# First layer of a two-layer image network: 42 of the 170 hidden channels get a TensorE pointwise product and nine VectorE depthwise taps, and the stacked rows are copied by DMA

## The reference, cut to what matters

```python
h = jnp.einsum('oi,bihw->bohw', w_in, x)             # 64 -> 3 * 170 channels
gate, x_sp, x_fr = jnp.split(h, 3, axis=1)
sp = conv_general_dilated(x_sp, w_dw, ..., padding='SAME', feature_group_count=170)   # 3x3, one filter a channel
f  = jnp.fft.rfft2(x_fr in 8x8 patches) * fft_weight
fr = jnp.fft.irfft2(f)
fused = jax.nn.gelu(gate) * (sp + fr)
out = jnp.einsum('oi,bihw->bohw', w_out, fused)      # 170 -> 64 channels, added to x
```

## Time and profile before

| what | value |
|---|---|
| time, median of 3 runs | 11264.19 us (11263.31 to 11265.12) |
| profiled execution, its own time | 11251.14 us |
| its span, first to last instruction | 11249.3 us |
| mean granted TensorE clock | 0.973 |
| TensorE matmuls busy | 10537.8 us (94%), 62242 instructions |
| VectorE busy | 7718.4 us (69%), 11335 instructions |
| ScalarE busy | 5114.5 us (45%) |
| GpSimd busy | 2503.7 us (22%) |
| DMA queue of SyncE | 1334.39 MB, 41.6% of 16 engines |

### The profile page before, as it was taken

One profiled execution on the slowest core, in us unless ns is written; L12 is line 12 of the kernel. 1 busy time (PEld: TensorE's weight loads), 2 busy tenths in 40 slices (PEclk: granted clock), 3 DMA queues, 4 the chain that ended last, 5 costly groups with the idle time before them and its releaser, 6 DMA issues.

```text
span 11249.3 us, 161094 instructions
## 1 busy us (share of the span) xinstructions
PE 10537.8 (94%) x62242; PEld 7829.9 (70%) x62242; DVE 7718.4 (69%) x11335; ACT 5114.5 (45%) x7799; POOL 2503.7 (22%) x2340
## 2 busy tenths in 40 slices
PE   1999998999899999998989999999998999999998
PEld 1777775767677776675767777667676777757666
DVE  6555558888655555897855555688884555578787
ACT  0333334656633333464753333445474333345557
POOL 0111112233211111323321111222332111122333
PEclk6999999999999999999999999999999999999999
DMA  4333325465533333546543333444563222253555
GB/s 124 62 74 63 71 57 209 158 225 144 133 71 63 75 64 103 185 158 224 146 114 63 70 64 73 144 160 182 187 169 72 56 58 53 55 191 147 203 165 149
DMA packets 1203095, 1344.68 MB, mean 120 GB/s; under 512 B 829196, under 2 KB 1062044, under 8 KB 1100060
## 3 DMA queue, kind: packets, MB, share of 16 engines
q1 hardware_dynamic: 1202332, 1334.39, 41.6%
HBM read 787.50 MB, written 515.26 MB: 116 GB/s over the span
## 4 chain that ended last, share of the span: by engine, by line
issue 42%; PE 37%; DVE 10%; POOL 8%; ACT 2%; DMA 1%; SPq 0%; POOLq 0%; DVEq 0%; ACTq 0%
PE ps L1637 12%; POOL xo L983 7%; PE ps L1650 6%; PE ps L1228 4%; PE ps L1664 3%; PE ps L1255 3%; DVE S L1426 3%; PE ps L1221 2%; PE ps L1659 2%; PE ps L1292 2%; DVE fp L1395 2%; DVE rs L1215 1%; DVE fx L1386 1%; ACT fp L1349 1%; PE ps L796 1%
## 5 line engine op out<-in xcount | busy, mean ns | idle before, releaser
L983 POOL TENSOR_SCALAR xo<-xo 64x512 f32<-64x512 f32 x504 | 783.6, 1578 | 4848.2 <-DVE xo L1078 4848.2
L904 ACT ACTIVATE XF<-ps 128x340 f32<-128x340 f32 x1024 | 465.6, 455 | 2865.4 <-PE ps L760 2865.3
L1637 PE MATMUL ps<-fp,Dwr 128*128 128x512 f32 x6144 | 1471.4, 389 | 0.0
L1637 PEld LDWEIGHTS ps<-fp,Dwr 128*128 128x128 f32 x6144 | 1153.4, 188 | 239.4
L1042 DVE TENSOR_TENSOR Z<-ps,LW 128x340 f32<-128x340 f32 x1024 | 524.3, 512 | 1105.5 <-PE ps L769 1097.8
L806 PE MATMUL ps<-P,WP 128*106 128x512 f32 x3072 | 934.7, 439 | 0.0
L796 PE MATMUL ps<-H,WP 128*128 128x512 f32 x3072 | 924.2, 423 | 0.0
L1078 DVE TENSOR_TENSOR xo<-ps,raw 64x512 f32<-64x512 f32 x512 | 351.9, 687 | 812.0 <-PE ps L849 808.5
L1228 PEld LDWEIGHTS ps<-RS,Bc 128*128 128x128 f32 x4096 | 570.6, 195 | 483.9 <-DVE RS L1217 241.5
L1228 PE MATMUL ps<-RS,Bc 128*128 128x128 f32 x4096 | 762.7, 310 | 144.2 <-DVE RS L1217 144.2
L1650 PE MATMUL ps<-XP,Cwr 128*128 128x512 f32 x3072 | 832.2, 408 | 68.1 <-DVE XP L1769 68.1
(11 more groups left out here) (294 smaller groups left out, 21146.5 us busy)
## 6 DMA issues: line engine op xcount, KB each, us to landing
raw<-x SPq DMA_DIRECT2D x240, 640.0 KB, 8.3
fx_d<-fx SPq DMA_DIRECT2D x112, 1024.0 KB, 3.9
fl_d<-fp SPq DMA_DIRECT2D x112, 1024.0 KB, 5.4
fp<-fl_d SPq DMA_DIRECT2D x112, 1024.0 KB, 6.1
fx<-fx_d SPq DMA_DIRECT2D x112, 1024.0 KB, 5.5
x1h_d<-xo SPq DMA_DIRECT2D x256, 256.0 KB, 8.3
x1v_d<-xo SPq DMA_DIRECT2D x512, 128.0 KB, 5.0
xin<-x1v_d SPq DMA_DIRECT2D x64, 1024.0 KB, 4.8
```

Source lines behind the costliest of these rows:

```text
L904: e.activation(XF[n % 2][:], ps[6][:, 0:2 * HID], ACT.Copy).then_inc(sem["xf"], 1)
L983: ins = e.tensor_scalar(dst, src, 1.0, None, ALU.mult)
L1637: ins = e.matmul(bank(m)[:], Dwr[:, w, c:c + 128], fq[n % 2][x][:, s2, :], start=(s2 == 0 and w == 0 and x == 0), stop=False)
```

## The change

The pointwise product of the 42 channels is no longer multiplied by the taps in advance. `pointwise` makes it once for the ten rows that a tile needs (nine rows of 130 columns in each half of the partitions): three pieces of 106 x 390, each of three matmuls, into PSUM banks 0, 1 and 5, which the gates use too. ScalarE copies them into a new SBUF tile `U` (`uc`). VectorE makes nine taps in `F42` (`depthwise`: one multiplication, then eight scalar_tensor_tensor that add onto the same tile, each of which waits for the one before). `finv42` has bank 4 for itself, and `fu42` becomes two instructions, the second waiting for the first: add the bank to `F42`, then multiply by the gate.

`pairs` is gone from VectorE. SyncE copies the two halves of `Hh` from `P` by two DMAs a tile (`load_h_rows`). `pointwise` of tile t + 1 stands in tile t, where `conv42` stood, and so do the first two blocks of the 128-channel `conv`, which need no `Hh`. On VectorE `p2(t + 2)` stands behind `fu42(t)`, and `bn` ahead of `z(t + 1, 3)`. The weights `WP` shrink from 1680 to 1150 columns.

```diff
+    def load_h_rows(e, b, t):
+        e.wait_ge(sem["p2"], NT * b + t + 1)
+        if t >= 2:
+            e.wait_ge(sem["gate42"], NT * b + t - 1)
+        for p in range(2):
+            e.dma_start(HH[t % 2][64 * p:64 * p + 64, :, :].bitcast(F32),
+                        PP[t % 2][0:64, :, 130 * p:130 * p + 1170].bitcast(F32)).then_inc(sem[f"h{t % 2}"], 16)
...
         def gate(t, i):
-            if t:
-                e.wait_ge(sem["ge"], 2 * (NT * b + t - 1) + i + 1)
+            e.wait_ge(sem["uc"], 3 * (NT * b + t) + i + 1)
...
-        def conv42(t, blocks):
...
+        def pointwise(t, k):
+            if k == 0:
+                h_there(e, b, t)
+            if t:
+                if k < 2:
+                    e.wait_ge(sem["ge"], 2 * (NT * b + t - 1) + k + 1)
+                else:
+                    e.wait_ge(sem["ge42"], NT * b + t)
+            for pw_, px in PARTS:
+                ins = e.matmul(ps[(0, 1, 5)[k]][0:106, 0:390], w(pw_, W_U, 106), HH[t % 2][:, px, 390 * k:390 * k + 390],
+                               start=(pw_ == 0 and px == 0), stop=(pw_ == 1))
...
         for t in range(NT):
             if t:
                 gate(t, 0)
                 gate(t, 1)
-                conv(t, 0, range(5))
+                conv(t, 0, range(2, 5))
             finv(t, 0)
             xs(t + 1, 0)
...
             fs(t + 1, 1)
-            conv42(t, range(3))
+            pointwise(t + 1, 0)
+            pointwise(t + 1, 1)
             xs(t + 1, 2)
             wout(t - 1)
             fs(t + 1, 2)
-            conv42(t, range(3, 6))
+            pointwise(t + 1, 2)
+            conv(t + 1, 0, range(1))
             xs(t + 1, 3)
             finv42(t)
+            conv(t + 1, 0, range(1, 2))
             fs(t + 1, 3)
...
+        def uc(t, k):
+            e.wait_ge(sem["um"], 3 * (NT * b + t) + k + 1)
+            e.activation(U[t % 2][:, 3 * k:3 * k + 3, :].rearrange("c r w -> c (r w)"), ps[(0, 1, 5)[k]][0:106, 0:390],
+                         ACT.Copy).then_inc(sem["uc"], 1)
...
+        def depthwise(t, taps):
+            o = F42[t % 2][:].rearrange("c (a w) -> c a w", a=4)
+            for i in taps:
+                y, x = divmod(i, 3)
+                u = U[t % 2][:, y:y + 7:2, x:x + 128]
+                if i == 0:
+                    e.wait_ge(sem["uc"], 3 * (NT * b + t) + 3)
+                    ins = e.tensor_scalar(o, u, wd[0:106, 0:1], None, ALU.mult)
+                else:
+                    e.wait_ge(sem["tap"], 9 * (NT * b + t) + i)
+                    ins = e.scalar_tensor_tensor(o, u, wd[0:106, i:i + 1], o, ALU.mult, ALU.add)
+                ins.then_inc(sem["tap"], 1)
...
         for t in range(NT):
             fu(t, 0)
             z(t + 1, 0)
+            depthwise(t, range(4, 7))
             fu(t, 1)
             z(t + 1, 1)
             fl42(t - 1)
             x1(t - 1)
+            depthwise(t, range(7, 8))
             z(t + 1, 2)
+            depthwise(t, range(8, 9))
...
+            bn(t - 1)
             z(t + 1, 3)
             if b + 1 < NB:
                 gn1_dve(e, b + 1, t)
+            fu42(t)
             p2(t + 2)
-            fu42(t)
-            pairs(t + 2)
-            bn(t - 1)
+            depthwise(t + 1, range(4))
```

More of the change, by code:

```diff
@@ L23 @@
 NW = 8
-W_CONV, W_C42, W_G42, W_GATE, W_FR, NWP = 0, 640, 1276, 1382, 1510, 1680
+W_CONV, W_U, W_G42, W_GATE, W_FR, NWP = 0, 640, 746, 852, 980, 1150
 SEMAPHORES = (
@@ L124, in build @@
     kc_d = dram("kc_d", [2, 2, 128, 4224])
-    lw_d = dram("lw_d", [128, 2340])
+    lw_d = dram("lw_d", [128, 1819])
     tb_d = dram("tb_d", [2, 128, 2048])
@@ L150, in build @@
     base = offset[0]
-    LW = at("LW", [128, 2340])
+    LW = at("LW", [128, 1819])
     base0 = offset[0]
[L155 to L158, removed]
+    cv128 = LW[:, W_CONV:W_U].rearrange("p (a b) -> p a b", a=5)
+    Wt, woA, wo42 = LW[:, NWP:1490], LW[:, 1490:1554], LW[0:106, 1554:1682]
+    ctr, wd = LW[:, 1682:1810], LW[:, 1810:1819]
     CC = at("CC", [128, 2, 4224])
@@ L215, in build @@
     raw = [at(f"raw{i}", [128, 10, 258]) for i in range(3)]
-    P = [[at(f"P{i}{p}", [128, 10, 130], F32R) for p in range(2)] for i in range(2)]
-    Hh = [[at(f"H{i}{p}", [128, 9, 130], F32R) for p in range(2)] for i in range(2)]
+    PP = [at(f"P{i}", [128, 2, 1300], F32R) for i in range(2)]
+    HH = [at(f"H{i}", [128, 2, 1170], F32R) for i in range(2)]
+    P = [[t[:, p, :].rearrange("c (r w) -> c r w", w=130) for p in range(2)] for t in PP]
+    Hh = [[t[:, p, :].rearrange("c (r w) -> c r w", w=130) for p in range(2)] for t in HH]
+    U = [at(f"U{i}", [106, 9, 130]) for i in range(2)]
     xb = [at(f"xb{i}", [128, 1024], F32R) for i in range(2)]
@@ L289, in meeting @@
         e.wait_ge(sem["met"], 4 * k)
-    LOADS = 25
+    LOADS = 26
     STORES = 11
@@ L557, in setup_pool @@
         e.wait_ge(sem["ld"], 16 * LOADS)
[L558 removed]
+        e.memset(LW[:, 0:1682], 0.0).then_inc(sem["LW0"], 1)
         e.wait_ge(sem["LW0"], 1)
@@ L565, in setup_pool @@
             own(e.tensor_tensor(cv128[hf, j, :], winT[hf, HID:HID + 128], wdw[hf, tap, 0:128], ALU.mult))
[L567 to L573, removed]
+        for hf, c in ((lo, W_U), (hi, W_U + 64)):
+            copy(LW[hf, c:c + HL], winT[hf, HID + 128:2 * HID])
         for hf, c in ((lo, W_G42), (hi, W_G42 + 64)):
@@ L695, in stv_there, with h_there @@
         e.wait_ge(sem[f"stv{st % 2}"], 64 * (16 * b + st // 2 + 1))
+    def h_there(e, b, t):
+        e.wait_ge(sem[f"h{t % 2}"], 32 * (32 * b + t // 2 + 1))
+    def load_h_rows(e, b, t):
+        if t >= NT:
+            return
+        e.wait_ge(sem["p2"], NT * b + t + 1)
[4 more added lines that the diff above has]
+                        PP[t % 2][0:64, :, 130 * p:130 * p + 1170].bitcast(F32)).then_inc(sem[f"h{t % 2}"], 16)
     def load_raw(e, b, st):
@@ L721, in l0_sp @@
             gn1_sp(e, b + 1, 0)
+        load_h_rows(e, b, 0)
+        load_h_rows(e, b, 1)
+        load_h_rows(e, b, 2)
+        load_h_rows(e, b, 3)
         for st in range(32):
@@ L779, in conv @@
         def conv(t, i, blocks):
+            if t >= NT:
+                return
             if blocks[0] == 0:
                 if i == 0:
-                    e.wait_ge(sem["h"], NT * b + t + 1)
+                    e.wait_ge(sem["p2"], NT * b + t + 1)
                 if t:
@@ L785, in conv @@
             col = 64 * i
+            if blocks[0] == 2 or i and blocks[0] == 0:
+                h_there(e, b, t)
             for j in blocks:
@@ L797, in conv @@
                              start=(j == 0 and pw_ == 0 and px == 0), stop=False)
-        def conv42(t, blocks):
[L800 to L809, removed]
+        def pointwise(t, k):
+            if t >= NT:
+                return
+            if k == 0:
+                h_there(e, b, t)
+            if t:
[6 more added lines that the diff above has]
+                               start=(pw_ == 0 and px == 0), stop=(pw_ == 1))
+            ins.then_inc(sem["um"], 1)
         def gate42(t):
-            if t:
-                e.wait_ge(sem["ge42"], NT * b + t)
+            e.wait_ge(sem["uc"], 3 * (NT * b + t) + 3)
             for pw_, px in PARTS:
@@ L828, in finv42 @@
             e.wait_ge(sem["z"], 4 * (NT * b + t) + 4)
+            if t:
+                e.wait_ge(sem["ad"], NT * b + t)
             R = Rinv[:].rearrange("k (a p c) -> k p a c", a=4, p=2)
@@ L832, in finv42 @@
                     o = ps[4][64 * p:64 * p + HL, :].rearrange("p (a c) -> p a c", a=4)
-                    ins = e.matmul(o[:, :, 16 * k:16 * k + 16], Z[t % 2][:, k, 128:HID], R[:, p], start=False,
-                                   stop=(k == 7), skip_group_check=True)
+                    ins = e.matmul(o[:, :, 16 * k:16 * k + 16], Z[t % 2][:, k, 128:HID], R[:, p], start=True,
+                                   stop=True, skip_group_check=True)
             ins.then_inc(sem["fi42"], 1)
@@ L854, in l0_pe @@
         xs(0, 0)
-        gate(0, 0)
-        gate(0, 1)
-        conv(0, 0, range(3))
+        conv(0, 0, range(2))
+        for k in range(3):
+            pointwise(0, k)
+        e.matmul(ps[4][0:106, :], w(0, W_U, 106), HH[0][:, 0, 0:512], start=True, stop=True)
         fs(0, 0)
-        conv(0, 0, range(3, 5))
+        conv(0, 0, range(2, 5))
         xs(0, 1)
@@ L864, in l0_pe @@
         xs(0, 2)
+        gate(0, 0)
+        gate(0, 1)
+        fs(0, 2)
         gate42(0)
-        fs(0, 2)
         xs(0, 3)
@@ L924, in fh42 @@
             e.activation(FP42[t % 2][0][:], F42[t % 2][:], ACT.Copy).then_inc(sem["fh42"], 1)
+        def uc(t, k):
+            if t >= NT:
+                return
+            e.wait_ge(sem["um"], 3 * (NT * b + t) + k + 1)
+            if t >= 2 and k == 0:
+                e.wait_ge(sem["tap"], 9 * (NT * b + t - 1))
+            e.activation(U[t % 2][:, 3 * k:3 * k + 3, :].rearrange("c r w -> c (r w)"), ps[(0, 1, 5)[k]][0:106, 0:390],
+                         ACT.Copy).then_inc(sem["uc"], 1)
```

(30 more changed lines are left out.)

4 lines of the change are left out of this document (3 added, 1 removed), and 4 rows, old and new, of the table SEMAPHORES.

## The result

The changed kernel takes 11889.76 us (median of 4 runs, 11881.03 to 11893.71) against 11263.81 us before: a ratio of 1.0554, with a 95% interval of 1.0536 to 1.0573. The forecast was 11790 us and slower. The profiled execution took 11881.03 us, 629.9 more than the one before. Each first layer became longer: from the first `xs` of an image to the last gate by 173.5, 172.2, 173.4 and 111.4 us, 630 us in all; the stretches between them changed by some 4 us at most, and by less than 1 us in sum.

What follows compares the result with a forecast made beforehand. The bound was taken to be a chain over VectorE and ScalarE back to TensorE, without slack. 192 tiles x 2.3 plus 64 x 1.3 gave 525 us on 11251, and 13 more for the median: 11790 us, range 11420 to 11920.

Steps and rivals of the forecast that it cites:

- The first piece: Tile from last fs to first xs: 5.75 us grows to 7.06, TensorE idling 2.75 us, since p2 stands behind fu42.
- The second piece: Tile from first xs to last fs: 15.78 us falls to 15.48, fewer matmuls but a new wait.
- The wait for `z`: Fourth xs waits for the third z, delayed by a tap ahead of it: 0.87 us (0.7 to 1.1).
- The clock: TensorE's granted clock falls behind first-layer stalls: 1.3 us a tile in three images, 0.9 in the last.
- The cost of a fall: TensorE at the 0.50 clock after a stall loses 1.5 us before the clock returns to 1.00.
- The share: The clock falls behind five of six stalls in the first three images.
- The ends: At the ends, a smaller load of weights against the wait for first stacked rows: nothing, within 15 us.
- the 9.3 us of cover: Time from p2's end until the first pointwise needs the stacked rows; copies taking 6 to 8 us stay hidden.
- That the clock holds: Rival: clock stays at 1.00 in the first layer, only waits count, 220 us more, 11485 us; chance 0.21.
- That TensorE's matmuls decide: Rival: xb and third z come in time, tile 18.92 us, 10596 us; chance 0.14 wholly or in part.

Runs made afterwards that it cites:

- the matmuls in the stall: Changed kernel plus eight unused 512-column matmuls on TensorE between finv (first half) and the first xs of each tile: 11517.32 us, ratio 1.0223.
- the last experiment: Changed kernel, p2 ahead of last z, tap 7 behind third z, first copies earlier, stacked rows ahead of raw and x1h: 10731.94 us, ratio 0.9531.
- short taps: Changed kernel with taps 1 to 8 made on only 4 of the 128 columns of each row: 11661.5 us, ratio 1.0351.
- both moves: Changed kernel with p2 ahead of the last z of the tile and tap 7 behind the third z: 10977.12 us, ratio 0.9743.

## Why the prediction was right

- **The first piece.** Forecast 7.06 us from `fs` to `xs` and 2.75 us of idling; measured 6.94 and, from start to start as the sum counts, 2.76 (810.50 to 814.07 less the 0.81 that finv took before the change, 812.37 to 813.18); the trace's 2.52 is counted from the modelled end of finv. The reading that decided it was the 0.07 us between `xb` and `xs` in the earlier trace rows; the old kernel with `fu42` first confirms it.
- **The second piece.** Forecast 15.48 us with the clock at 1.00. With p2 ahead of fu42, where the clock stays, it is 15.59 us. The wait for `z` is 0.67 as the trace counts it, behind the modelled end of the conv block, and 0.83 from start to start, where 0.87 was forecast: the `xs` starts 2.77 us behind the `fs` (801.89 to 804.66), and TensorE's own work there is 1.94 (0.42 for the `fs`, 0.80 for the three of 390 columns, 0.72 for the three of 512). The first piece came out 0.12 us shorter than forecast and the second 0.11 longer, so that their sum is right to 0.01 us in part by luck.
- **The clock.** The cost of a fall was right (1.5 us forecast, 1.58 measured by the matmuls in the stall). The share was not: five of six were taken, with two stalls to go by, and all tiles fell in three images. Those 0.28 us in 192 tiles are about half of the 100 us that the forecast was short. In the last image 1.3 us a tile were forecast and 1.6 came, 20 us more: 0.44 of waits, near the forecast 0.4 (21.95 with the matmuls in the stall, less 21.51), and 1.2 of the clock instead of 0.9.
- **The ends.** Forecast at nothing, within 15 us. The first stacked rows of an image are waited for 13.1 us in the first image and 7.0 in the last. Over what 64 tiles of 2.56 us more (1.62 in the last image) come to, the images lost 8 to 10 us each: some 35 us. The sum had the 9.3 us of cover of a tile inside an image, and at the start there is none.
- **The rivals.** That the clock holds is refuted by the 0.50 behind every stall of images 1 to 3. The rule on idle gaps in the Trainium skill (TensorE: Matmul & The Clock Gate, "HAM oscillation — how this bites in real kernels") would let a stall of 2.52 us pass; here it cost the clock in every tile of three images, and the measurement decides. That TensorE's matmuls decide is nearly true in the last experiment alone: 19.31 us against the 18.92 of that rival's sum, with some 0.3 us of the chains between the two. Of VectorE's taps only tap 7 showed, ahead of the `z` that is waited for, as said.

## What to carry to other kernels

A busy row of 100% does not say that an engine's work is the bound: at each instruction that waits for another engine, look for a chain over the other engines that ends at the same moment. Removing work under such a chain turns into idling, and what is put ahead of a link costs nearly its whole length (0.54 us of 0.60 in the kernel before). So when work moves to another engine, place it behind whatever that engine hands to the bound one, and issue the transfers it needs ahead of those with time to spare. Then look at the clock: here 2.5 us of idling in each tile cost another 1.6 us, and filling the gap with unneeded matmuls gave it back.

## What the runs showed of the hardware that was not expected

- With stalls of 2.52 us in tiles of 24 us the clock fell in 183 of 183 tiles, although of two stalls of 2.5 us before the change one cost the clock and one did not; with 1.2 us of idling it fell in none. In the last image, with 1.9 us, it fell in 47 of 61. With short taps, where the stall is 2.51 us and the tile 23.3, it fell in some 150 of 183, so the length of the stall alone does not tell; what else decides is not shown.
- A dependent chain of scalar_tensor_tensor on one tile costs little more than its parts: three taps that wait for each other take 2.33 us together, 0.75 each, and the first tap, a tensor_scalar, 0.48.
- The time to landing of a copy depends on what is ahead of it in the queue. With both moves the two copies of 585 KB landed after 9.0 and 10.9 us where they were issued 2.65 us behind two stores of x1h and two loads of raw, and after 5.0 and 7.4 us where nothing had been issued for some 10 us; in the last experiment they land after 5.0 to 5.2 and 7.4 to 7.8 us everywhere.
